# Two transformer layers on one core: quartered local probes, two fillers in two pipelines, and value product, output projection and projection put behind one another over a ring of four banks

## The reference

```python
# layer 0, attention: 32 heads, 8 of keys, 8 wide; three branches, mixed by gates
fsim = einsum('bhgnd,bhnjd->bhgnj', rq, fk) * SCALE      # selected blocks of 16 keys
...
# local: windows of 64, each query sees its own and the window before, at most 64 keys back
smask = (delta >= 0) & (delta <= WIN)
ssim = where(smask, einsum('bhgwid,bhwjd->bhgwij', qw, kcat) * SCALE, NEG)
s_out = einsum('bhgwij,bhwjd->bhgwid', softmax(ssim), vcat)
...
# layer 1, attention (2 softmaxes in a row, the second over scores + cam_bias)
# layer 1, ffn: has an attention of its own, then 16 experts
h = rms(x, ln_w)
q, k, v = rope(h @ wq), rope(h @ wk), h @ wv     # 32 heads, 8 of keys, 64 wide
attn = softmax(where(causal, q @ k.T / 8, -1e30))
x = x + (attn @ v) @ wo
h = rms(x, ff_ln_w); gate = softmax(top4(h @ wg)); ...
```

## Time and profile before

| what | value |
|---|---|
| median of 3 runs | 4583.56 us (4581.97 to 4587.42) |
| the profiled execution, its time | 4580.2 us |
| its span | 4578.3 us, 83656 instructions |
| TensorE busy | 3971.1 us, 87% |
| VectorE busy | 3145.4 us, 69% |
| ScalarE busy | 2061.8 us, 45% |
| GpSimd busy | 1522.2 us, 33% |
| phase A | 110 to 1758 us |
| phase BC | 1758 to 2400 us |
| phase D | 2400 to 4065 us |
| phase E | 4065 to 4578 us |

### The profile page before, as it was taken

One profiled execution on the slowest core, in us unless ns is written; L12 is line 12 of the kernel. 1 busy time (PEld: TensorE's weight loads), 2 busy tenths in 40 slices (PEclk: granted clock), 3 DMA queues, 4 the chain that ended last, 5 costly groups with the idle time before them and its releaser, 6 DMA issues.

```text
span 4578.3 us, 83656 instructions
## 1 busy us (share of the span) xinstructions
PE 3971.1 (87%) x28830; PEld 2316.6 (51%) x28831; DVE 3145.4 (69%) x9004; ACT 2061.8 (45%) x4817; POOL 1522.2 (33%) x1291
## 2 busy tenths in 40 slices
PE   6898989899898996998868789898989989859995
PEld 3444445444444444775533344444444444439995
DVE  6777777777777782567746586867677776755555
ACT  1353645353544553332225455555555555534442
POOL 0010101010100102334016465656465655645553
PEclk7899999898999998999989999999999999979998
DMA  5122122221211205862127521212121111145666
GB/s 121 21 33 45 28 41 35 35 37 31 44 31 28 34 15 178 266 205 80 47 67 109 70 64 39 65 41 62 42 61 45 49 58 40 57 152 103 112 106 167
DMA packets 320363, 327.79 MB, mean 72 GB/s; under 512 B 161062, under 2 KB 253630, under 8 KB 318814
## 3 DMA queue, kind: packets, MB, share of 16 engines
q1 hardware_dynamic: 275898, 250.27, 21.7%
q0 software_dynamic: 39936, 70.87, 9.0%
q10 hardware_dynamic: 4112, 1.29, 0.2%
HBM read 182.56 MB, written 92.94 MB: 60 GB/s over the span
## 4 chain that ended last, share of the span: by engine, by line
PE 65%; DVE 23%; ACT 3%; issue 3%; DMA 3%; POOL 2%; SPq 1%; ACTq 0%; DVEq 0%; POOLq 0%
PE PS L2291 7%; PE PS L2813 6%; PE PS L2342 5%; PE PS L2357 4%; PE PS L850 4%; PE PS L2306 3%; DVE a_mm L1246 3%; DVE PS L2624 3%; PE PS L2824 3%; PE PS L790 3%; PE PS L817 3%; PE PS L2326 2%; PE PS L828 2%; PE PS L1754 2%; PE PS L636 2%
## 5 line engine op out<-in xcount | busy, mean ns | idle before, releaser
L1246 DVE TENSOR_REDUCE a_mm<-PS 128x4 f32<-128x512 f32 (+3 forms) x960 | 605.3, 649 | 289.3 <-PE PS L794 253.1
L2698 POOL TENSOR_TENSOR d_ef<-d_ef,d_soft 128x768 f32<-128x768 f32 (+3 forms) x512 | 637.8, 1256 | 356.5 <-DVE d_soft L2633 354.0
L999 ACT ACTIVATE a_PT<-PS 128x512 f32<-128x512 f32 x896 | 512.6, 602 | 503.2 <-PE PS L828 341.5
L2405 ACT ACTIVATE d_ef<-PS,d_soft 128x128 f32<-128x128 f32 (+3 forms) x1024 | 530.3, 525 | 259.5 <-DVE d_soft L2633 192.9
L2624 DVE CUSTOM_DVE_ANT_0 PS<-PS,d_cmask 128x128 f32<-128x128 f32 (+3 forms) x1024 | 481.1, 511 | 219.4 <-PE PS L2326 189.5
L2306 PE MATMUL PS<-W 64*128 64x128 f32 (+3 forms) x2048 | 413.6, 481 | 75.0 <-ACT d_ef L2405 57.5
L2416 ACT ACTIVATE d_tf<-PS 128x512 f32<-128x512 f32 (+1 forms) x384 | 201.9, 526 | 399.2 <-PE PS L2326 398.4
L2342 PE MATMUL PS<-d_tf,W 128*64 128x512 f32 x1280 | 325.6, 641 | 13.8 <-DVE d_tf L2642 13.0
L1453 POOL DMA_INDIRECT list<-a_tok,slots x64 | 63.3, 989 | 817.0 <-ACT a_PT L999 788.6
L2326 PEld LDWEIGHTS PS<-ident,d_ef 64*128 64x128 f32 x5120 | 221.2, 144 | 215.6 <-issue 70.0
L2326 PE MATMUL PS<-ident,d_ef 64*128 64x64 f32 x5120 | 238.8, 231 | 103.3 <-ACT d_tf L2416 47.0
(11 more groups left out here) (389 smaller groups left out, 7873.3 us busy)
## 6 DMA issues: line engine op xcount, KB each, us to landing
W<-W SPq DMA_DIRECT2D x768, 64.0 KB, 2.0
W<-in_exp SPq DMA_DIRECT2D x96, 384.0 KB, 4.8
e_xg<-xrow SPq DMA_DIRECT2D x144, 132.5 KB, 2.1
a_Q<-scr SPq DMA_DIRECT2D x384, 32.0 KB
yrow<-bc_ob SPq DMA_DIRECT2D x48, 256.0 KB, 5.5
W<-in_exp SPq DMA_DIRECT2D x16, 768.0 KB, 10.0
scr<-a_qsp SPq DMA_DIRECT2D x24, 384.0 KB, 3.0
acc<-in_zero POOLq DMA_DIRECT2D x34, 256.0 KB, 11.6
```

Of the source, the lines that this page charges most:

```text
L999: e.activation(PT[:, 4 * (n % 2) + q4, :], RS.of(("exp", n, q4))[:, :], ACT.Exp, scale=S0).then_inc(act.sem, act.mark(("exp", n, q4)))
L1246: e.tensor_reduce(mm[:, i % 2, kind, c:c + len(gs)], RP.of(("top", b, u, kind, gs[0]))[:, 0:len(gs) * n].rearrange("p (g k) -> p g k", g=l ...
L2405: e.activation(ef[:, n % 7, r, 0:nk], S.of(("exp", n))[:, r, 0:nk], ACT.Exp, scale=-1.0, bias=nm[:, n % 7, r:r + 1], accum_out=zz[:, n % 7 ...
L2698: e.tensor_tensor(ef[:, n % 7, :, 0:nk], ef[:, n % 7, :, 0:nk], zr[:, n % 7, :].unsqueeze(2).to_broadcast([128, 2, nk]), ALU.mult).then_in ...
```

## The change

In phase A the mask table is changed, the local probe for i > 0 is done in four quarters of 32 queries x 96 keys each, and VectorE's maximum goes over 96 keys per head. A local probe is placed at the same fraction of its step as the step's first `multiply`. The transposes `hT`, their copies and the load of the next batch's keys come two small pieces later, and the number of small pieces that a batch has is raised to match. The layer norm's last three passes become two. In BC there is one empty piece ahead of the value product `o` and one behind it, on the engines that have a share in it, and two more steps at the end. In D `projects` moves from n % 4 == 1 to n % 4 == 3, `out_proj` from n % 4 == 0 to n % 4 == 2, right behind `times`, and `collect` to n % 4 == 3; `out_proj` takes its bank from `TX`, which has four; and some entries of `late` move by one or two units.

```diff
     k = np.arange(256)
...
-    c["smask"] = sm[:, 64:].astype(bf)
+    quarter = p[:, None] % 32 + 64 - np.arange(96)[None]
+    quarter = np.where((quarter >= 0) & (quarter <= 64), 0.0, NEG)
+    c["smask"] = np.concatenate([sm[:, 128:], quarter], 1).astype(bf)
...
             for i in rows:
                 chain(e, dve)
-                e.tensor_scalar(dst[:, i, :], X(4 * b + i), mv[:, i, 0:1], rs[:, 2, i:i + 1], ALU.subtract, ALU.mult
-                                ).then_inc(dve.sem, dve.tick())
+                e.scalar_tensor_tensor(dst[:, i, :], X(4 * b + i), mv[:, i, 0:1], mb[:, 1, :], ALU.subtract, ALU.mult
+                                       ).then_inc(dve.sem, dve.tick())
                 chain(e, dve)
-                e.tensor_tensor(dst[:, i, :], dst[:, i, :], mb[:, 1, :], ALU.mult).then_inc(dve.sem, dve.tick())
-                chain(e, dve)
-                e.tensor_tensor(dst[:, i, :], dst[:, i, :], mb[:, 0, :], ALU.add
-                                ).then_inc(dve.sem, dve.mark(("norm", b)))
+                e.scalar_tensor_tensor(dst[:, i, :], dst[:, i, :], rs[:, 2, i:i + 1], mb[:, 0, :], ALU.mult, ALU.add
+                                       ).then_inc(dve.sem, dve.mark(("norm", b)))
...
-                    want = (2.2 * (u + 1) if u < 15 else 33 + 30 * (u - 14) / 15) if b < 8 else 0
+                    want = (2.2 * (u + 1) if u < 15 else 33 + 32 * (u - 14) / 15) if b < 8 else 0
                     parts = math.ceil(max(want - ran, 0))
                     ran += parts
                     looks = [(probe, b, u, *look) for look in probes(u // 8)] if b < 8 else []
                     order = [(k / parts, side.piece) for k in range(parts)]
-                    for each in (work, looks):
-                        order += [((k + 0.5) / len(each), *w) for k, w in enumerate(each)]
+                    order += [((k + 0.5) / len(work), *w) for k, w in enumerate(work)]
+                    beside = [w[0] for w in order if w[1] is multiply]
+                    for k, w in enumerate(looks):
+                        local = w[3] == 1 and beside
+                        order.append((beside[0] if local else (k + 0.5) / (len(looks) - bool(beside)), *w))
                     for w in sorted(order, key=lambda w: w[0]):
...
                 def prepare(b):
                     y = b % 2
-                    for _ in range(8):
+                    for _ in range(10):
                         yield
                     e.wait_ge(dve.sem, dve.at(("kv", b)))
                     e.dma_start(D["kvs"], kv[:]).then_inc(c_kv.sem, c_kv.mark(("kv", b), 16))
...
-                    yield
-                    yield
-                    yield
-                    yield
+                    for _ in range(6):
+                        yield
                     pe_columns(e, pe, dve, act, RM, "hT", (dve, ("norm", b)), h, b)
...
                     if kind and i:
                         for g in gs:
-                            for x in range(2):
-                                k0 = 128 * i - 64 + 64 * x
-                                e.matmul(p[64 * x:64 * x + 64, 128 * g:128 * g + 128],
-                                         Q6[0:96, 4 * hh + g, k0 + 64:k0 + 128],
-                                         K6[0:96, y, kind, hh, k0:k0 + 128], start=(g == 0), stop=False)
-                        for x in range(2):
-                            e.matmul(p[64 * x:64 * x + 64, :].rearrange("p (g k) -> p g k", g=4),
-                                     identb[:, 64 * x:64 * x + 64],
-                                     smask[:, 64 * x:64 * x + 128].unsqueeze(1).to_broadcast([128, 4, 128]),
+                            for x in range(4):
+                                q0 = 128 * i + 32 * x
+                                e.matmul(p[32 * x:32 * x + 32, 96 * g:96 * g + 96],
+                                         Q6[0:96, 4 * hh + g, q0:q0 + 32],
+                                         K6[0:96, y, kind, hh, q0 - 64:q0 + 32], start=(g == 0), stop=False)
+                        for x in range(4):
+                            e.matmul(p[32 * x:32 * x + 32, 0:384].rearrange("p (g k) -> p g k", g=4),
+                                     identb[:, 32 * x:32 * x + 32],
+                                     smask[:, 128:224].unsqueeze(1).to_broadcast([128, 4, 96]),
                                      start=False, stop=True).then_inc(pe.sem, pe.mark(("top", b, u, kind, gs[0])))
...
-                    n = 128 if kind else 128 * i + 128
+                    n = (96 if i else 128) if kind else 128 * i + 128
...
-                for s in range(92):
+                for s in range(94):
...
                     yield from turn(n, 1)
+                    yield
                     turned(n, 1)
...
                         yield
+                    yield
                     pe_columns(e, pe, dve, act, R, "oT", (dve, ("o", n, 1)), o, n)
...
-            TX = Ring([PS[:, 4, :], PS[:, 5, :], PS[:, 6, :]])
-            Y = PS[:, 7, 0:256]
+            TX = Ring([PS[:, 4, :], PS[:, 5, :], PS[:, 6, :], PS[:, 7, :]])
...
             for b in range(-1, 8):
-                n = 64 * b + 1
+                n = 64 * b + 3
...
-            late = {-22: ("x2", 0), -1: ("square", 0), 3: ("square", 1), 7: ("square", 2), 11: ("square", 3),
-                    12: ("h2root", 0), 14: ("h2", 0), 15: ("h2", 1), 16: ("HT", 0), 17: ("gate", 0),
+            late = {-20: ("x2", 0), 0: ("square", 0), 4: ("square", 1), 8: ("square", 2), 12: ("square", 3),
+                    13: ("h2root", 0), 14: ("h2", 0), 15: ("h2", 1), 16: ("HT", 0), 17: ("gate", 0),
...
                 for n in range(9 * N):
+                    if n >= 15 and n % 4 == 3 and (n - 15) // 4 < 2 * N:
+                        collect((n - 15) // 4)
                     if n < 8 * N:
...
-                    if n >= 12 and n % 4 == 0 and (n - 12) // 4 < 2 * N:
-                        out_proj((n - 12) // 4)
                     if n >= 14 and n % 4 == 2 and (n - 14) // 4 < 2 * N:
-                        collect((n - 14) // 4)
+                        out_proj((n - 14) // 4)
...
                 def out_proj(J):
                     b, hp, i, _, _ = unit(4 * J)
-                    if J:
-                        e.wait_ge(dve.sem, dve.at(("y", J - 1)))
-                    else:
+                    p, old = TX.take(dve, ("y", J))
+                    vacate(e, old)
+                    if J == 0:
...
-                    e.tensor_tensor(y, y, Y, ALU.add).then_inc(dve.sem, dve.mark(("y", J)))
+                    e.tensor_tensor(y, y, TX.of(("y", J))[:, 0:256], ALU.add).then_inc(dve.sem, dve.mark(("y", J)))
```

More of the change, by code:

```diff
@@ L792, in probe @@
                     w = n if kind else 128
-                    mask = smask[:, 192 - n:192] if kind else cmask[:]
+                    mask = smask[:, 0:128] if kind else cmask[:]
                     e.matmul(p[:, 0:n * len(gs)].rearrange("p (g k) -> p g k", k=n)[:, :, n - w:n], identb[:],
@@ L1083, in prepare @@
                         gates(1)
-                    yield
-                    yield
-                    yield
+                    for _ in range(5):
+                        yield
                     dve_columns(e, pe, dve, RM, "hT", hT, 0, b)
@@ L1430, in prepare @@
                 def prepare(b):
-                    for _ in range(19):
+                    for _ in range(21):
                         yield
@@ L1559, in main @@
                 def main(n):
-                    for _ in range(20):
+                    for _ in range(22):
                         yield
@@ L1793, in main @@
                     yield from turn(n, 1)
-                    yield
-                    yield
+                    for _ in range(4):
+                        yield
                     act_columns(e, pe, act, R, "oT", oT, 0, n)
@@ L2356, in out_proj @@
                             at = 128 * g + 64 * x
-                            e.matmul(Y[64 * x:64 * x + 64, :], oT[:, J % 2, at:at + 64], wo[:, hp, g, :],
+                            e.matmul(p[64 * x:64 * x + 64, 0:256], oT[:, J % 2, at:at + 64], wo[:, hp, g, :],
                                      start=(g == 0), stop=(g == 3)).then_inc(pe.sem, pe.mark(("out", J)))
```

2 lines of the change are left out of this document (1 added, 1 removed).

## The result

The changed kernel takes 4689.0 us (median of four, 4677.5 to 4695.8) against 4585.5 us of the kernel before, measured beside it: ratio 1.0221, interval 1.0196 to 1.0245. It is slower, by 103 us; 4672 was forecast. The profiled execution has a span of 4686.0 us, 107.7 above the 4578.3 of before.

A forecast was written before the change was run, and what follows sets the result against it. TensorE's own order of work, with short waits, was taken as the bound. D's +133 at full clock, +55 for clock, A's -80 and BC's -20 gave +88 us, put on the median 4672 us; range 4520 to 4790.

The forecast's parts named there:

- The scores' loop: D: without long blocks between, S1 and S2 wait for exponentials, 275 us in place of 57.5.
- The ring's waits: D: with four banks, TensorE's waits for copies (`d_tf`) go, -60 us.
- V's tile changes: D: V's block loses its two changes between 64-row and 128-row tiles in each of 128 groups, -25 us.
- The norm's pieces: D: the layer norm's pieces move by one step at most, costed at nothing.
- The clock in D: D: new holes lower TensorE's granted clock for the work behind them, +55 us, bounds 0 and 163.
- The probe: A: 16 matmuls of 96 columns and 4 masks replace the halves' 8 and two; with the value product's row, -20 us.
- Rival 2: Dear probes at 30 ns per short matmul, and D's clock falls in half of its holes: 4752 us, chance 0.24.
- The place: A: the local probe right behind a value product saves two tile changes in 192 steps, -25 us.
- hT: A: transposes asked for two pieces later remove TensorE's 29.3 us wait for the norm, -25 us with clock.
- BC: Two fillers let TensorE do other batches' work during waits of 19.2 and 16.7 us, -20 us.
- Rival 3: A's clock rises to 0.96 as its holes close: faster, 4474 or some 4510 us, chance 0.18.
- Rival 4: D's two effects cancel and A's gain pays for the clock: within 9 us of 4584, chance 0.06.

The follow-up runs named there:

- d_p_apart: D's part of the change on the kernel before, but with the projections left at n % 4 == 1: 4561.0 us, ratio 0.9949.
- d_mul_later: d_only with VectorE's second multiplication of a q or k projection moved behind the next unit's maximum: 4779.1 us, ratio 1.0432 against the kernel before.
- d_s3: d_only with three double banks for scores and two banks for everything else: 4967.5 us, ratio 1.0841 against the kernel before.
- d_norm: D's part of the change and the shorter layer norm, on the kernel before: 4689.6 us, ratio 1.0227.
- d_only: D's part of the change alone, on the kernel before: 4730.5 us, ratio 1.0326.
- best2: Kernel before plus quartered probe in its old place, shorter norm, BC's fillers, and D's ring of four with the old order: 4474.4 us, ratio 0.9760.
- ring4_old_order: Kernel before with D's ring of four banks, the output projection's bank taken from it, VectorE's sum one unit earlier, TensorE's order kept: 4529.8 us, ratio 0.9888.

## Why the prediction was right, and where it was not

The time came out 17 us above the forecast and well inside the range. The mechanism in D was right; that the number came so near is luck, since two terms were wrong by over 60 us each, with opposite signs.

- **The scores' loop** ("and what decides"): right in mechanism and in place. The maximum of unit 3 starts at the 1.29 us of the walk; d_p_apart and d_mul_later each touch one link of the loop and move the holes as it says, and d_s3 fits it. The size was too large. Against holes of 2.3 us with 512 keys there are 1.98 (1.47 and 0.51), for 2.2 there are 1.86 (1.67 and 0.19), for 2.6 there are 2.06, for 1.5 there are 0.97 (0.52 and 0.45): 6.9 a round, not 8.6. Mostly the second hole was mis-sized: with its 0.7 us in each of 128 groups the walk has 90 us of second holes and 185 of first ones, and the trace has 63.9 and 182.8. All of D's waits for `d_ef` are 246.8 us where 275 stood, since holes longer than the typical ones come on top.
- **The ring's waits** (-60): from 67.4 us, of which the forecast left a row of 7.4 out, to 22, so -45. Alone, with the old order, the fourth bank gives 49 us, but half of that is busy time.
- **V's tile changes** (-25): a V of 16 matmuls went from 3.58 to 3.48 us start to start and an O from 1.78 to 1.73, 0.15 a group, -19.
- **The norm's pieces** ("costed at nothing since they are the same"): wrong. TensorE's wait for `f_h` is 40.7 us. The row of TensorE's waits in D of the kernel before:

```profile
PE PS L2243 <- DVE f_h L2450: 19.1, 8, 4.4
```

  It doubled. Of the 15 waits seven are new, of 0.4 to 1.5 us, ahead of the transposes of the next batch's norm, and seven went from 2.1 to 4.2 us at the unit where `late` has the batch's second norm. These passes (L2450) are not the ones that the change shortened, and in d_norm the wait is 43.0 us.
- **The clock in D** (+55, bounds 0 and 163): about +18 in the full change (busy time level, of which 19 us were saved), about +48 in d_only. The forecast took a third of 96 stretches at half clock on top of those before; D has 50 of them (273 us) where it had 25 (189 us). The size depends on the length of the norm's passes (d_norm), which I had not seen.
- **The probe** (-20 and part of VectorE's -10): right, -27 measured. Rival 2 fell: sixteen short matmuls take 0.17 us, 11 ns each, about a quarter of the 40 ns that the forecast gave to 96 columns, so four column tiles do run at once, as in the value product. The Trainium skill (TensorE: Matmul & The Clock Gate, "Wait — 56ns, not 53.3ns?") says that matmuls never start less than about 25 ns apart, however small. That and the estimate of +19 from it do not hold for these tiles; the measurement decides.
- **The place** (-25): nothing measurable. The change of tiles is saved, and given back in holes and clock; why they come isn't shown.
- **hT** (-25): the step that failed most, +34. I took a wait with one reason away and wrote down its length as the gain. "VectorE's backlog stays" stood in the text, but not what it would do: four other waits stand where the one stood, and the clock fell.
- **BC** (-20): -13 in the full change, -16 in best2, some 3 of it the shorter norm's.

D 64 us below its term and A 75 us above its own nearly cancel. Of the signs for being right, D's was narrowly missed (+124 where 130 to 190 stood) and A's altogether. Rival 3 (A's clock to 0.96) did not come: it fell to 0.91. Rival 4 neither.

## What to carry to other kernels

Before long blocks are put together to save tile changes, count for each ring how much work stands between a buffer's use and its next one: the long blocks were the cover, spread by the old order over two places of the group, and bunching them over the ring of four cost 200 us (4730 against 4530) to save 19. A spare bank should be tried with the order left alone; here it was worth 49 us. A wait named after one producer isn't the price of that producer: move the consumer and look at which wait comes next, and size a change made of many parts by running each, since here four gains (bank, probe, norm, fillers) and two losses (the order in D, the shift in A) were sent out as one.

## What the runs showed that I had not expected

- Matmuls of 96 columns on 32-column tiles run at 11 ns each, sixteen in 0.17 us, four masks of 384 columns in 0.28, their change of tiles included.
- The same 12369 instructions of TensorE in D were busy for 1483 to 1641 us, from the ring of four to d_s3, with the granted clock at 0.95 and 0.86. With the clock, waits lengthen work that isn't waiting; the fourth bank that cut TensorE's idle time by 26 us cut its busy time by 24 too (ring4_old_order).
- A square root between exponentials costs ScalarE two loads of 1.28 us.
